# Two transformer layers with routed experts: gathers without the wait for the gate table, the fourth expert's weights before the stores, and the last blocks written out

## What is computed

```python
router = softmax(xf @ gate_w + gate_b)            # 1536 x 8
k_scores, k_idx = top_k(router, 2)
comb = zeros((t, e)).at[arange(t)[:, None], k_idx].add(k_scores)
for i in range(e):
    h = silu(xf @ w1[i] + b1[i])                  # 256 -> 1024
    out = out + (h @ w2[i] + b2[i]) * comb[:, i:i + 1]
```

## Time and profile before

| | |
|---|---|
| time, median of 3 runs | 612.24 us (607.44 to 615.18) |
| the profiled execution: time | 610.04 us |
| its span | 607.7 us (2.3 us of its time lie outside) |
| mean granted TensorE clock | 0.956 |
| busy: PE, PEld | 547.5 us (90%), 480.5 us (79%) |
| busy: DVE, ACT, POOL | 333.5, 335.6, 288.3 us |
| the attention stage of the first layer | about 0 to 72 us |
| its experts' blocks, from the first x_transpose to the landing of the last scatter | 88.95 to 300.87 us |
| the second layer's, likewise to its last scatter's issue | 390.29 to 600.95 us |

### The profile page before, as it was taken

One profiled execution on the slowest core, in us unless ns is written; L12 is line 12 of the kernel. 1 busy time (PEld: TensorE's weight loads), 2 busy tenths in 40 slices (PEclk: granted clock), 3 DMA queues, 4 the chain that ended last, 5 costly groups with the idle time before them and its releaser, 6 DMA issues.

```text
span 607.7 us, 15574 instructions
## 1 busy us (share of the span) xinstructions
PE 547.5 (90%) x3570; PEld 480.5 (79%) x3571; DVE 333.5 (55%) x729; ACT 335.6 (55%) x608; POOL 288.3 (47%) x346
## 2 busy tenths in 40 slices
PE   8999767999999999997959997699999999999962
PEld 4887326999999899996638873389999999999962
DVE  6558873456534555562185578644566564655420
ACT  5785514566655667664166754245666566665530
POOL 4648041455654466564354350434556555554432
PEclk9999989999999999999769999799999999999985
DMA  8533686356532553325162207822364464222110
GB/s 287 148 97 73 208 299 213 76 139 153 124 57 40 143 128 58 88 35 161 32 217 66 76 5 259 310 82 42 90 165 133 120 177 118 43 72 44 31 26 9
DMA packets 48568, 70.54 MB, mean 116 GB/s; under 512 B 9048, under 2 KB 39968, under 8 KB 48544
## 3 DMA queue, kind: packets, MB, share of 16 engines
q1 hardware_dynamic: 34272, 55.87, 28.7%
q0 software_dynamic: 10944, 14.17, 13.5%
q10 hardware_dynamic: 3328, 0.20, 0.3%
HBM read 57.54 MB, written 13.73 MB: 117 GB/s over the span
## 4 chain that ended last, share of the span: by engine, by line
PE 66%; DMA 12%; DVE 7%; issue 5%; ACT 3%; POOL 3%; SPq 1%; POOLq 1%; DVEq 0%; ACTq 0%
PE banks L1185 16%; PE banks L1187 15%; PE banks L1186 15%; PE banks L1393 6%; PE banks L1224 5%; DMA seed_rows<-in_L_ffn_b_dram 3%; DMA expert_io<-xn_dram,gcol 3%; DVE stats L831 2%; PE banks L1362 2%; PE banks L1298 2%; DMA mid_dram<-expert_io,scol 1%; DMA xres<-in_x_dram 1%; PE banks L1235 1%; DVE xres L969 1%; DMA out_dram<-expert_io,scol 1%
## 5 line engine op out<-in xcount | busy, mean ns | idle before, releaser
L1185 PE MATMUL banks<-w_hi,hT_hi 128*128 (+2 forms) x392 | 119.2, 304 | 6.1 <-DVE hT_lo L1147 6.1
L1185 PE MATMUL banks<-w_hi,xT_hi 128*128 x336 | 119.6, 356 | 5.4 <-DVE xT_lo L1088 3.4
L1187 PE MATMUL banks<-w_hi,xT_lo 128*128 x336 | 115.0, 342 | 0.0
L1186 PE MATMUL banks<-w_lo,xT_hi 128*128 x336 | 114.5, 341 | 0.0
L1187 PE MATMUL banks<-w_hi,hT_lo 128*128 (+2 forms) x392 | 114.1, 291 | 0.0
L1186 PE MATMUL banks<-w_lo,hT_hi 128*128 (+2 forms) x392 | 114.0, 291 | 0.0
L760 ACT COPY banks<-seed_rows 128x1024 f32 (+1 forms) x58 | 66.8, 1151 | 35.4 <-SPq L421 31.0
L1185 PEld LDWEIGHTS banks<-w_hi,hT_hi 128*128 128x128 f32 (+2 forms) x392 | 78.0, 199 | 8.0 <-issue 6.5
L563 POOL TENSOR_TENSOR w_lo<-raw,w_hi 128x1024 fp32r<-128x1024 f32 (+1 forms) x24 | 60.4, 2539 | 47.8 <-ACT w_hi L639 47.8
L1186 PEld LDWEIGHTS banks<-w_lo,hT_hi 128*128 128x128 f32 (+2 forms) x392 | 78.5, 200 | 0.0
L583 POOL DMA_INDIRECT expert_io<-xn_dram,gcol x56 | 56.8, 1015 | 45.7 <-POOL gcol L579 43.6
(11 more groups left out here) (196 smaller groups left out, 915.7 us busy)
## 6 DMA issues: line engine op xcount, KB each, us to landing
raw<-in_L_ffn_w_dram SPq DMA_DIRECT2D x32, 512.0 KB, 3.9
raw<-in_L_ffn_W_dram SPq DMA_DIRECT2D x16, 672.0 KB, 4.0
raw<-in_L_ffn_W_dram SPq DMA_DIRECT2D x16, 336.0 KB, 3.8
seed_rows<-in_L_ffn_b_dram SPq DMA_DIRECT2D x8, 672.0 KB
seed_rows<-in_L_ffn_b_dram SPq DMA_DIRECT2D x8, 512.0 KB
xn_dram<-raw SPq DMA_DIRECT2D x6, 512.0 KB, 3.0
xres<-in_x_dram SPq DMA_DIRECT2D x3, 512.0 KB, 4.5
wqkv<-in_L_conv_W_qkv_dram SPq DMA_DIRECT2D x2, 768.0 KB, 5.6
```

The source lines that it names most:

```text
L1185: pe.matmul(out, hi, w_high, start=first, stop=False, skip_group_check=onto)
L1186: pe.matmul(out, hi, w_low, start=False, stop=False, skip_group_check=onto)
L1187: return pe.matmul(out, lo, w_high, start=False, stop=last, skip_group_check=onto)
```

## The change

Five edits, all around the blocks of the experts:

1. POOL waits for the gate table in scatter(0), no longer ahead of its loop.
2. SP issues expert 3's weights before the six stores, and the bias row of expert 0 alone; it signals that one, then loads those of experts 1 and 2. `load_conv(1)` moves behind the load of expert 4.
3. `block_loop` gets a number `lead`: so many steps before the last one are taken out of the guarded loop and written out (one on ACT and DVE, two on POOL). They are called with `ahead=False` and leave out what is for blocks that don't exist: the gathers of blocks 28 and 29, their split and seed, and the pieces of weights.
4. PE no longer transposes the block of padding, reads the numbers of the last two experts before its first block, and has four matmuls on zeros between h_transpose(blocks-1) and second_product(blocks-1).
5. DVE writes the last block's rows to `xg`, and POOL scatters them from there (`last_scatter`), without the copy to `y_out`, with its row numbers in `gcol`. In the second layer SP waits for the last scatter by itself.

```diff
@@ block_loop
-            steps(eng, 2, 0, blocks, step)
-            step(blocks, last=True)
+            steps(eng, 2, lead, blocks, step)
+            for n in range(lead, 0, -1):
+                step(blocks - n, ahead=False)
+            step(blocks, ahead=False, last=True)
@@ SP
+                load_expert(L, SLOTS, 0)
                 dst = (mid_dram, out_rows)[L].rearrange("(i p) c -> p i c", p=P)
...
-                load_expert(L, SLOTS, 0)
                 sp.wait_ge(s.store, 6 * 16)
-                for e in range(SLOTS):
+                load_seed(L, 0)
+                seed_loaded()
+                for e in range(1, SLOTS):
                     load_seed(L, e)
-                for e in range(SLOTS):
+                for e in range(1, SLOTS):
                     seed_loaded()
                 expert_loaded(L, 0)
+                sp.wait_ge(s.gathered, 16)
+                load_expert(L, SLOTS + 1, 1)
+                expert_loaded(L, 1)
                 if L == 0:
 
                     load_conv(1)
                     sp.wait_ge(s.lg, 1)
                     load_route(1)
-                sp.wait_ge(s.gathered, 16)
-                load_expert(L, SLOTS + 1, 1)
-                expert_loaded(L, 1)
...
-            sp.wait_ge(lay[1].moe_done, 1)
+            sp.wait_ge(lay[1].tab, 2)
+            sp.wait_ge(lay[1].added, 16 * block_count(sp))
+            sp.sem_inc(lay[1].moe_done, 1)
@@ POOL
                 def scatter(b):
                     if after(b, 1):
                         pool.wait_ge(s.added, 16 * b)
+                    else:
+                        pool.wait_ge(s.tab, 3)
...
-                pool.wait_ge(s.tab, 3)
-
-                def step(b, last=False):
-                    if not last:
+
+                def last_scatter(b):
+                    pool.wait_ge(s.gathered, 16 * b)
+                    pool.tensor_copy(gcol[:, :], col(scatter_tab, b)).then_inc(s.scol, 1)
+                    pool.wait_ge(s.scol, b + 1)
+                    pool.wait_ge(s.e_sb, b + 1)
+                    pool.wait_ge(s.added, 16 * b)
+                    pool.sem_inc(rows_go, 1)
+                    pool.indirect_dma_start(out=acc, out_offset=bass.IndirectOffsetOnAxis(ap=gcol[:, :], axis=0),
+                                            in_=xg, in_offset=None, bounds_check=TOKENS - 1,
+                                            oob_is_err=False, compute_op=ALU.add).then_inc(s.added, 16)
+
+                def step(b, ahead=True, last=False):
+                    if ahead:
                         gather(b + 2)
-                    if after(b, 1):
+                    if last:
+                        last_scatter(b - 1)
+                    elif after(b, 1):
                         scatter(b - 1)
-                    if last:
+                    if last and L == 0:
                         pool.wait_ge(s.added, 16 * b)
-                        pool.wait_ge(s.gathered, 16 * b + 16)
                         pool.sem_inc(s.moe_done, 1)
 
-                block_loop(pool, step)
+                block_loop(pool, step, 2)
@@ ACT (DVE likewise)
+                    if not ahead:
+                        return
...
-                block_loop(act, step, s.tab)
+                block_loop(act, step, 1, s.tab)
@@ DVE
-                    if not last:
+                    if ahead:
                         xT_low(b + 1)
...
+                        rows = xg if last else y_sb(b - 1)
...
-                block_loop(dve, step, gates=gates)
+                block_loop(dve, step, 1, gates=gates)
@@ PE
                 blocks = block_count(pe)
+                e_old, e_last = expert_of(blocks - 2), expert_of(blocks - 1)
                 x_transpose(0)
...
                 steps(pe, 2, 1, blocks, step)
-                e_old, e_last = expert_of(blocks - 2), expert_of(blocks - 1)
-                x_transpose(blocks)
                 second_product(blocks - 2, e_old)
                 h_transpose(blocks - 1)
+                keep_busy(BUSY_LAST, 3)
                 second_product(blocks - 1, e_last)
```

24 lines of the change are left out of this document (12 added, 12 removed).

## The result

| | kernel before | changed kernel |
|---|---|---|
| time, median | 611.54 us (607.44 to 615.18, 4 runs) | 594.65 us (592.52 to 596.51, 4 runs) |
| the profiled execution: time, span | 610.04, 607.7 us | 592.52, 590.8 us |
| mean granted TensorE clock | 0.956 | 0.972 |
| busy PE | 547.5 us | 541.2 us |

The ratio is 0.9725 with a 95% interval of 0.9651 to 0.9798: 2.75% faster. 597.0 us was forecast, in a range of 591 to 605.

A forecast was written before the change was run, and what follows sets the result against it. Loops are bound by PE, so gains come only from openings and ends: 5.2 + 1.1 + 4.3 + 3.6 = 14.2 us, giving 595.8 from 610.04 or 598.0 from 612.24; forecast 597.0, range 591 to 605.

The forecast's parts named there:

- the clock term of the first opening: First layer, step after x_transpose(2): PE idles under 1 us, keeps 2.4 GHz, 6.72 instead of 8.28 us; 1.5 us gained.
- Opening of the first layer: First layer's first blocks: earlier seed 0.3, earlier gather(2) 3.7, kept clock 1.5; 5.2 us gained (3.1 to 5.4).
- Rival B: First opening: gather(2) stays late beside expert 4's load and the clock falls; opening gives 2.6, time 599.5 us; chance 10%.
- Rival C: Both openings: gather(0) and PE's zeros end as late as the seeds did; openings give 4.9 and 0.3, 598 us; 8%.
- Opening of the second layer: Second layer's first blocks: early seed gives 1.0, gather(2) 0.1; 1.1 us gained (0.4 to 1.5).
- End of the first layer: First layer's last blocks: POOL's chain is the later one, last scatter at 293.2 instead of 297.73; 4.3 us (3.0 to 5.0).
- They move one block forward, where DVE has to wait for PE in any case: First layer's end: DVE's 2.46 us of issue, taken as empty passes, falls where DVE idles 2.31 us before the gate product.
- By that the zeros hold the clock: First layer's end: without the four matmuls on zeros the product ends 2.4 us later and the sum is 0.7 less.
- End of the second layer: Second layer's last blocks: last scatter starts at 595.8 instead of 599.38; 3.6 us gained (2.7 to 4.6).
- PE restarts second_product(26) after 2.01 us of issue, at the low clock, and that stays: Second layer's end: issue and low clock remain; only 0.5 us given for dropped transposes and number loads.
- A, the landings decide: Both ends: POOL's scatter chain falls further behind, each end gives 1.5; 9.3 us in all, time 602; chance 20%.
- D, slower by code that must be fetched: Loop exits and written-out steps, five per layer end, cost 2.01 us each: 20 us in all, time 617; chance 4%.

The follow-up runs named there:

- the experiment with the openings alone: Kernel before with the moved gate wait and SP's new load order, old ends kept; ratio 0.9883 (0.9838 to 0.9927) to the kernel before.
- the experiment with the ends alone: Changed kernel with the gate wait and SP's load order of the kernel before; ratio 0.9847 (0.9799 to 0.9895) to the kernel before.
- the repetition: The changed kernel measured once more, with nothing altered; 593.82 us, ratio 0.9756 (0.9709 to 0.9803) to the kernel before.
- the gate wait alone: Kernel before with one edit, POOL waiting for the gate table in scatter(0) instead of ahead of its loop; ratio 0.9962 (0.9920 to 1.0005).
- the loads alone: Kernel before with only SP's load order of the changed kernel; ratio 1.0008 (0.9974 to 1.0042) to the kernel before.

## Why the prediction was right, and where its steps were not

**The sum.** 14.2 us were forecast; the spans differ by 16.9 (607.7 less 590.8). By ratio the two measurements of the changed kernel give 2.75% and 2.44%, which is 16.8 and 14.8 us. The forecast is near all three, but in part by luck: the clock term of the first opening and the end of the second layer were worked out from one profile's low clock, which not all executions show, as said below. Openings: 6.3 forecast, 7.1 by the experiment with the openings alone (4.5 to 9.9). Ends: 7.9 forecast, 9.3 by the experiment with the ends alone (6.4 to 12.2).

**Opening of the first layer: right.** POOL's copy within 0.3 us of x_transpose(1): 0.07. x_transpose(2) at 99.78, forecast 99.7. Idle under 1 us and the clock kept. But the 1.5 us for the clock belong to the profile that they were worked out from: with the same old opening, in the experiment with the ends alone, the clock stayed up over 3.12 us idle, and the old opening took 20.54 us instead of 22.70. "Nobody wants it for 200 us", of `load_conv(1)`, was looked at from the load's side only. Beside loads a gather can be long: in the repetition gather(3), with `load_conv(1)` just issued, lasted 6.13 us and the opening 18.12, and without the zeros gather(2) lasted 4.92 and the opening 18.80, while the opening takes 17.25 in the profiles in which PE waits for no gather. That is up to 1.5 us left on the table. Rival B did not come true here: gather(2) took 4.23 us, about as long as it asked, but PE idled only 0.68 us and kept its clock. Rival C, that the seeds weren't the bound, is true in some executions: in six of fourteen profiles x_transpose(0) came only at 91.2 to 91.9 (the last section says how), and the chain of the one among them that has the old order of the seeds (ends alone) doesn't run through the bias rows.

**Opening of the second layer: 1.1 forecast, 1.0 in the stage table, but split otherwise.** The seed was put at 1.0 and gather(2) at 0.1. From x_transpose(0) to (1) 0.6 us are gained (7.14 to 6.54), and from (1) to (2) 0.3 (6.44 to 6.10); the gate wait alone gives 0.7, the loads alone 0.4. The 0.9 us ahead of the opening is no gain that can be told: with the load of the next weights in its old place that stretch is 88.1 to 89.4 us, in kernels of either order.

**End of the first layer: right in mechanism and size.** 4.3 forecast, 5.2 between the two profiles, 3.6 when the old end is taken from three other profiles. POOL's chain was named as the later one, with the last scatter 0.8 us behind a landing. Two parts of the reasoning fell without changing the sum. "They move one block forward, where DVE has to wait for PE in any case": there PE does stand idle, 0.46 us before second_product(26), and POOL's chain covers it. The row names DVE's `hT_lo`; PE shows the same 0.46 us as issue in the second layer, so its own three passes may be the cause. Without empty passes on any engine the 0.46 us is gone in both layers. "By that the zeros hold the clock" was drawn from the Trainium skill (TensorE: Matmul & The Clock Gate, section What's actually happening), by which activity releases the throttle. It stood against 1.46 us of idle time in the earlier trace rows, which already said that PE keeps its clock over such a gap. Without the zeros PE idles 1.22 us and keeps it. The row was right, and the 0.7 us credited to the zeros are none.

**End of the second layer: the step that failed.** "PE restarts second_product(26) after 2.01 us of issue, at the low clock, and that stays". It didn't stay: 0.46 us of issue, and the high clock. The sum gave 0.5 us to the transposes and the number reads together, and the first layer's part put the 2.01 us down to the three empty passes, but the experiment that moves the two number reads back behind the loop brings 2.05 us and the low clock back. So the reads alone are 1.6 us, and the passes are the 0.46, which went when they went. The end gained 5.7 us between the profiles; 1.6 to 2.1 of that was the first profile's low clock through the whole end, which three other profiles of the old end had only in part. By the other profiles it is 3.8, near the 3.6 forecast; the term was near for executions in general and too small for the one that it was worked out from. SP's wait was put "below 0.3"; no run shows a gain by it.

**Rivals.** A, the landings decide: true of the mechanism in the first layer (a 7.3 us landing under the next layer's load), but it was in the forecast's sum already. D, slower by code that must be fetched: five written-out pieces per end would have cost 10 us. Apart from the passes ahead of them none shows more than 0.5 us of issue; what costs are passes that jump over a body, and there are as many as before. The Trainium skill (Runtime: NRT & Kernel Launch, section Instruction fetch mechanics) says that a taken branch out of the fetched window waits for a fetch, while straight code is fetched ahead. That would fit the empty passes of the first layer, 0.7 us each with a body and under 0.1 without, and the straight code behind them, which cost nothing that the traces show; that a fetch is what the passes wait for, no run shows.

## What to carry to other kernels

When a wait is removed, look at what else is late by the same amount, and at what the freed transfer will now run beside: here neither half of the opening gave a measurable gain alone, and together they gave 7 us (4.5 to 9.9). Read numbers that steer the last blocks before the loop, not behind it, and count a guarded pass as a cost even if it does nothing. Before a local gain is booked, take the same stretch from several profiles; one profile's end was 1 to 2 us off in each layer.
